# A fused block of sparse attention and routed experts: the order of statistics, masks, sums and weight pieces in its per-batch stage

## What is computed

```python
def xattn(h, adj, Wq, Wk, gamma_raw):                  # per batch, h = ctx, adj = layernorm(x)
    sim = einsum('bhnd,bhmd->bnm', Q, K) / (sqrt(32) * 4)
    threshold = top_k(sim, int(512 * 0.3))[0][:, :, -1:]   # the 153rd largest of each row
    A = sigmoid(sim) * (sim >= threshold)
    A = (A + swapaxes(A, -1, -2)) * 0.5
    gamma = sigmoid(gamma_raw)
    return (1.0 - gamma) * adj + gamma * A

x = x + tanh(g_xattn[0]) * xattn(ctx_512, layernorm(x), Wq, Wk, gamma_raw)
x = x + tanh(g_ffn[0]) * ffn(layernorm(x))     # shared silu(g) * y @ dw.T, and 2 of 8 experts by routing
```

## Time and profile before

| | us |
|---|---|
| median of 3 runs | 595.46 (594.64 to 596.95) |
| the profiled execution | 595.18 |
| its span, first to last instruction | 593.4 |
| attention of batch 0, up to the first shared block | 80.7 |
| stage of batch 1 | 62.0 |
| expert tiles | 258.7 |

### The profile page before, as it was taken

One profiled execution on the slowest core, in us unless ns is written; L12 is line 12 of the kernel. 1 busy time (PEld: TensorE's weight loads), 2 busy tenths in 40 slices (PEclk: granted clock), 3 DMA queues, 4 the chain that ended last, 5 costly groups with the idle time before them and its releaser, 6 DMA issues.

```text
span 593.4 us, 11085 instructions
## 1 busy us (share of the span) xinstructions
PE 507.4 (86%) x3169; PEld 289.1 (49%) x3170; DVE 343.6 (58%) x708; ACT 262.0 (44%) x473; POOL 232.2 (39%) x226
## 2 busy tenths in 40 slices
PE   2402589979998999879998899999999999999992
PEld 0100354434444454344464466666666666666660
DVE  0589758787868786977974377533333333333330
ACT  1696588646774579433231156322222222222221
POOL 1147735462446434550233034343343343443422
PEclk9655769989998999997999799999999999999997
DMA  3235293205611472034004489545445445445333
GB/s 113 97 91 173 80 305 108 57 30 182 250 42 36 138 275 57 21 106 147 1 1 159 149 230 242 123 77 95 79 75 95 78 78 96 74 77 97 74 43 46
DMA packets 32050, 63.75 MB, mean 107 GB/s; under 512 B 4049, under 2 KB 4305, under 8 KB 32017
## 3 DMA queue, kind: packets, MB, share of 16 engines
q1 hardware_dynamic: 23280, 42.89, 22.1%
q0 software_dynamic: 8736, 20.45, 18.9%
HBM read 41.05 MB, written 22.28 MB: 107 GB/s over the span
## 4 chain that ended last, share of the span: by engine, by line
PE 58%; DVE 17%; ACT 9%; issue 7%; DMA 5%; POOL 2%; SPq 1%; DVEq 1%; POOLq 0%; ACTq 0%
PE py L1004 12%; PE pg L984 12%; PE pu L985 12%; PE pg L845 4%; PE pu L845 4%; PE pt_bank L804 3%; DVE w L1178 3%; DVE pa L1137 3%; DVE w L1108 2%; PE pa L994 2%; PE py L862 2%; ACT w L613 2%; ACT w L619 2%; PE pu L862 2%; DVE w L1141 1%
## 5 line engine op out<-in xcount | busy, mean ns | idle before, releaser
L984 PE MATMUL pg<-w,x_t 128*128 x468 | 140.7, 313 | 0.0
L985 PE MATMUL pu<-w,x_t 128*128 x468 | 140.7, 313 | 0.0
L541 POOL DMA_INDIRECT out<-rows,idx x39 | 61.8, 1584 | 142.3 <-ACT rows L744 134.6
L1004 PE MATMUL py<-w,work 128*128 x351 | 82.1, 379 | 0.8 <-DVE work L1435 0.8
L845 PE MATMUL pg<-w 128*128 128x512 f16 (+1 forms) x288 | 80.2, 389 | 1.9 <-DVE work L1231 1.9
L845 PE MATMUL pu<-w 128*128 128x512 f16 (+1 forms) x288 | 79.7, 387 | 0.0
L734 ACT ACTIVATE work<-pg 128x352 f32<-128x352 f32 x39 | 18.0, 463 | 135.2 <-PE pu L985 135.2
L580 ACT ACTIVATE w<-stage 128x544 f16<-128x544 f32 (+1 forms) x80 | 50.7, 647 | 34.8 <-DMA stage<-in_weights 34.6
L488 POOL TENSOR_TENSOR w<-stage,w 128x544 f16<-128x544 f32 (+1 forms) x43 | 54.0, 1264 | 27.4 <-ACT stage L584 25.5
L494 POOL TENSOR_TENSOR work<-work 128x512 f16<-128x512 f32 (+1 forms) x24 | 29.0, 1209 | 81.9 <-ACT work L649 81.9
L1424 DVE SCALAR_TENSOR_TENSOR work<-pu,work 128x352 f32<-128x352 f32 x39 | 20.5, 524 | 62.6 <-ACT work L734 62.5
(11 more groups left out here) (189 smaller groups left out, 760.8 us busy)
## 6 DMA issues: line engine op xcount, KB each, us to landing
stage<-in_weights SPq DMA_DIRECT2D x80, 272.0 KB, 3.1
w<-in_x SPq DMA_DIRECT2D x4, 1024.0 KB, 6.6
out<-w SPq DMA_DIRECT2D x16, 256.0 KB, 2.8
xn_rows<-w SPq DMA_DIRECT2D x16, 256.0 KB, 5.3
out<-rows SPq DMA_DIRECT2D x13, 256.0 KB, 3.2
rows<-out SPq DMA_DIRECT2D x12, 256.0 KB, 3.0
w<-in_ctx_t SPq DMA_DIRECT2D x4, 256.0 KB, 3.4
out<-rows,idx POOLq DMA_INDIRECT x39, 4.7
```

The source lines that it names most:

```text
L541: pool.indirect_dma_start(out=out, out_offset=bass.IndirectOffsetOnAxis(ap=idx[:, t:t + 1], axis=0), in_=rows[:, t % 2, :], in_offset=None ...
L984: pe.matmul(pg[p][:, 0:H], lhs, w[:, item, half, at:at + H], start=begin, stop=end)
L985: mm = pe.matmul(pu[p][:, 0:H], lhs, w[:, item, half, at + H:at + 2 * H], start=begin, stop=end)
L1004: mm = pe.matmul(py[:, :], hid_t[:, p, part * JC + j, :], w[:, item, half, at:at + C], start=(j, part, half) == (0, 0, 0), stop=(j, part) ...
```

## The change

- **x.** Two buffers `xbs`, one of them in the place of weights item 6 (not yet loaded then), used by batch number. `load_x(1)` is issued behind `load_context(1)`, ahead of piece 8, the later ones behind the next context.
- **Masks.** They go to a buffer `kept` of their own, and ahead of the check for missed rows; the repair does its masks again. One release (`a_made`) per batch.
- **Sums.** `add_attention` is gone from POOL; DVE adds `kept` to x in `attended`.
- **x statistics.** `x_stats` comes behind the search in batch 0, and behind the first `shared_hidden` in the stages; `base` behind the searches, in the stages one block later than before.
- **Rows.** `statistics` of the sums and `row_scalars` by two tiles; ScalarE makes the high part in one pass straight from x, DVE the exact rows (`exact`) itself. DVE copies turned tiles 0 and 2, ScalarE 1 and 3.
- **Pieces.** `BY_DVE = 8`: DVE keeps 3 and 7 of the first 24. ScalarE does 16 pieces ahead of batch 0's rows instead of 20, and 8 behind `score_tanh(1)` instead of 4. POOL has `guess(1)` behind piece 17. PE waits for pieces as it needs them.
- **Loops.** The loop over the first two stages is written out on all engines.

```diff
-BY_DVE = 20
+BY_DVE = 8
-        xb = attn_tiles()
+        beside = w[:, EARLY - 1, :, :].rearrange("p b c -> p (b c)").bitcast(F32)
+        xbs = [beside[:, 0:TPB * SEQ].rearrange("p (i c) -> p i c", i=TPB), attn_tiles()]
+        kept = beside[:, TPB * SEQ:2 * TPB * SEQ].rearrange("p (i c) -> p i c", i=TPB)
...
             load_context(1, TPB)
+            load_x(1)
             for k in range(CHUNKS, last):
                 load_piece(k // CHUNKS, k % CHUNKS)
             sp.wait_ge(pad_st, 32)
             store_attended(0)
             store_rows(0)
-            load_x(TPB)
             load_piece(last // CHUNKS, last % CHUNKS)
... POOL
             first_pieces(0, FIRST)
-            add_attention(0)
-            first_pieces(FIRST, FIRST + 3)
-            row_scalars(0)
-            first_pieces(FIRST + 3, FIRST + 6)
+            row_scalars(0, 0)
+            row_scalars(0, 1)
+            first_pieces(FIRST, FIRST + 4)
             guess(1)
... POOL, stages
-                base_scalars(b + 1)
                 for u in range(UPS):
                     shared_low(b, u)
+                    if u == 1:
+                        base_scalars(b + 1)
                     if u < TPB:
                         low_piece(b + BEFORE, u)
-                add_attention(b + 1)
... ACT
             for n in range(ROUNDS):
                 count(0, n)
-                if n:
-                    base(0, (n - 1,))
                 high_piece(n // CHUNKS, n % CHUNKS)
-            base(0, (TPB - 1,))
-            for k in range(ROUNDS, FIRST + RING):
+            base(0)
+            for k in range(ROUNDS, FIRST + 2):
                 high_piece(k // CHUNKS, k % CHUNKS)
-            scores_and_rows(0, True, range(FIRST + RING, FIRST + RING + 2))
-            for k in range(FIRST + RING + 2, BEFORE * CHUNKS):
+            scores_and_rows(0, True)
+            for k in range(FIRST + 2, BEFORE * CHUNKS):
...
-                    if u == ROUNDS - 2:
+                    if u == ROUNDS - 1:
                         base(b + 1)
... DVE
+                for i in range(TPB):
+                    o.mark(keep(i))
                 after(dve, miss_mm, b + 1)
                 o.then(dve.tensor_copy(missed_i[:], pa[0][0:1, 0:1]))
...
+                for i in range(TPB):
+                    o.mark(dve.tensor_tensor(xbs[b % 2][:, i, :], kept[:, i, :], xbs[b % 2][:, i, :], ALU.add))
...
+                for i in (0, 2):
+                    if i:
+                        after(dve, xn_lo, b * TPB + i)
+                    made = [exact(i), exact(i + 1)]
+                    low_rows(i, made[0])
+                    low_rows(i + 1, made[1])
+                    if i == 0 and more:
+                        score_stats(b + 1, (0, 1))
+                    rows_turned(b, i)
...
             score_stats(0, range(TPB))
-            x_stats(0)
             for n in range(ROUNDS):
                 search(0, n)
+            x_stats(0)
             low_piece(0, 3)
...
-            masks(0, (1, 3))
-            low_piece(1, 7)
+            masks(0)
... DVE, stages
-                x_stats(b + 1)
                 search(b + 1, 0)
                 for u in range(UPS):
                     shared_hidden(b, u)
+                    if u == 0:
+                        x_stats(b + 1)
```

More of the change, by code:

```diff
@@ L385, in together @@
                 store_shared(tile0, 3)
-            with sp.Fori(0, BATCHES - 2) as b:
-                together(b, True)
-            together(BATCHES - 2, False)
+            for b in range(BATCHES - 1):
+                together(b, b + 2 < BATCHES)
             load_item(LATE)
@@ L525, in together @@
                 o.clear()
-            with pool.Fori(0, BATCHES - 2) as b:
-                together(b, True)
-            together(BATCHES - 2, False)
+            for b in range(BATCHES - 1):
+                together(b, b + 2 < BATCHES)
             for u in range(UPS):
@@ L649, in shared_high, with scores_and_rows @@
                 act.activation(hid_tb[0:m, u, 0, :], hb[0:m, u % 2, :], ACT.Copy).then_inc(hhi_sb, 1)
-            def scores_and_rows(b, more, pieces=()):
+            def scores_and_rows(b, more):
                 if more:
                     keep_qk(b + 1)
-                for k in pieces:
-                    high_piece(k // CHUNKS, k % CHUNKS)
                 for i in range(TPB):
@@ L703, in together @@
                 scores_and_rows(b + 1, more)
-            with act.Fori(0, BATCHES - 2) as b:
-                together(b, True)
-            together(BATCHES - 2, False)
+            for b in range(BATCHES - 1):
+                together(b, b + 2 < BATCHES)
             def router_exp():
@@ L832, in logits, with pieces_ready @@
                 mm.then_inc(lg_mm, 1)
+            def pieces_ready(n):
+                for r_, s in enumerate(w_lo):
+                    after(pe, s, len(range(r_, n, RING)))
+                after(pe, w_hi, n)
             def shared_up(b, u, beside=None, ks=range(KC)):
                 half, off, m = PIECES[u]
+                if b == 0 and 0 in ks and off == 0:
+                    pieces_ready(half * CHUNKS + -(-UP_W // CHUNK_W))
                 if u == 1 and beside is not None:
@@ L851, in shared_down @@
                 bank_ = down_bank(b, i)
+                if b == 0 and 0 in pieces and i == 0:
+                    pieces_ready(HALVES * CHUNKS)
                 if 0 in pieces:
@@ L878, in _ @@
                 turn_batch(0, i)
-            for s in w_lo:
-                after(pe, s, HALVES * (CHUNKS // RING))
-            after(pe, w_hi, HALVES * CHUNKS)
             pe.wait_ge(gw_ok, 1)
@@ L909, in together @@
                 turn_batch(b + 1, 3)
-            with pe.Fori(0, BATCHES - 2) as b:
-                together(b, True)
-            together(BATCHES - 2, False)
+            for b in range(BATCHES - 1):
+                together(b, b + 2 < BATCHES)
             def ranks():
@@ L1077, in low_piece, with statistics @@
                                          op0=ALU.mult, op1=ALU.subtract).then_inc(w_lo[n % RING], 1)
-            def statistics(s):
+            def statistics(s, tiles=range(TPB)):
                 o.wait()
-                for i in range(TPB):
+                for i in tiles:
                     o.mark(dve.bn_aggr(mv[:, s, i, :], bn6[:, s, i, :]))
@@ L1151, in count_missed, with masks, keep @@
                 o.then(dve.tensor_reduce(thr[:], hot8, AX.X, ALU.add))
-            def masks(b, piece=None):
+            def masks(b):
+                after(dve, sig_sb, (b + 1) * TPB)
+                after(dve, at_mm, b * TPB)
+                def keep(i):
+                    return dve.scalar_tensor_tensor(out=kept[:, i, :], in0=sim[:, i, :], scalar=thr[:, i:i + 1], in1=att[:, i, :],
+                                                    op0=ALU.is_ge, op1=ALU.mult)
+                for i in range(TPB):
+                    o.mark(keep(i))
                 after(dve, miss_mm, b + 1)
                 o.then(dve.tensor_copy(missed_i[:], pa[0][0:1, 0:1]))
-                if piece is not None:
-                    low_piece(*piece)
                 any_missed = dve.value_load(missed_i[0:1, 0:1], min_val=0, max_val=P * TPB)
@@ L1175, in masks @@
                         f.then(dve.tensor_copy(thr[:, i:i + 1], top8[:, i, (KEEP - 1) % 8:(KEEP - 1) % 8 + 1]))
-                after(dve, sig_sb, (b + 1) * TPB)
-                for i in range(TPB):
-                    dve.scalar_tensor_tensor(out=att[:, i, :], in0=sim[:, i, :], scalar=thr[:, i:i + 1], in1=att[:, i, :],
-                                             op0=ALU.is_ge, op1=ALU.mult).then_inc(a_made, 1)
+                        f.then(keep(i))
+                dve.sem_inc(a_made, 1)
             def attended(b, more, shared):
@@ L1273, in together @@
                 attended(b + 1, more, b)
-            with dve.Fori(0, BATCHES - 2) as b:
-                together(b, True)
-            together(BATCHES - 2, False)
+            for b in range(BATCHES - 1):
+                together(b, b + 2 < BATCHES)
             def bc(col):
```

144 lines of the change are left out of this document (73 added, 71 removed).

## The result

The changed kernel takes **621.03 us** (median of 4, 619.61 to 622.05) against 596.21 for the kernel before in the same rounds: ratio 1.045, 95% interval 1.041 to 1.050. It is slower by 4.5%, as forecast (616.0, range 604 to 626). Its profiled execution took 621.6 us.

The account below looks back on a forecast made before the run. Before 80.70 us TensorE mostly waits, and whatever moves the expert tiles' start moves the end. Third block 16.2 plus batches' 1.5, 1.1 and 2.0 gave 20.8, on 595.2: 616.0 us, range 604 to 626.

Parts of the forecast that it names:

- the head: Batch 0 up to its first transposes: late x statistics delay piece 7's low part by 7.0 us, the transposes by 6.5.
- From these transposes to the up-projection: Batch 0: 19.9 us instead of 18.7, so the up-projection starts at 88.4, 7.7 us late.
- the sums: Four new sums on VectorE in batch 0: 2.7 us, 1.5 of them beside the first transposes, so +1.2.
- I count nothing for all that together, bounds -2 and +2: Batch 0's rows: row scalars by halves, single-pass high rows, exact rows and score statistics together change nothing, within 2 us.
- The third block: Third up-block of batch 0: piece 23 waits behind eight stores, so it starts at 110.1 instead of 93.94, 16.2 us late.
- stores don't hold piece 23: Rival at the third block: it comes 10 us late instead of 16.2, 610 us in all; chance 0.15.
- The rounds of batches 1 to 3: Stages of batches 1 to 3: moved statistics, base activations, masks and sums cost +1.5, +1.1 and +2.0 us.
- the sums meet GpSimd: Rival in batches 2 and 3: GpSimd's pieces slow VectorE's sums, 4 us per batch, 624 us in all; chance 0.12.
- part 4: Rounds of batches 1 to 3: statistics +3.5, base activations -2.8 and +1.6, masks and check -0.8; batch 1 +1.5 us.
- The rule on exact rows: VectorE's exact rows: float32 tensor_scalar makes two results per cycle, so four take about 1.5 us instead of 3.

Follow-up runs that it names:

- e1: The changed kernel with x's statistics for batch 0 ahead of the four search rounds again: 611.33 us, ratio 1.030 to the kernel before.
- e7: e4 with the statistics of the first two score tiles behind the low rows of tiles 2 and 3: 599.97 us, ratio 1.008 to the kernel before.
- e2: The changed kernel with SyncE issuing weight piece 23 ahead of batch 0's eight stores: 615.16 us, ratio 1.039 to the kernel before.
- e3: The changed kernel with the weight pieces in their old places on ScalarE and GpSimd, x's statistics still late: 610.36 us, ratio 1.030.
- e10: The changed kernel with only the four sums of x and masked scores back on GpSimd: 612.68 us, ratio 1.031 to the kernel before.
- e5: e4 with the stages' old order: x's statistics and GpSimd's scalars at the head, base activations one block earlier: 594.71 us, ratio 1.000.
- e9: e4 with e5's order and e8's sums, so all costly moves undone: 585.53 us, ratio 0.984 to the kernel before.
- e12: e9 with the check of missed rows ahead of the four masks again, masks still in their own buffer: 591.5 us, ratio 0.996.
- e4: The changed kernel with e1 and e3 together: 600.04 us, ratio 1.010 to the kernel before.
- e8: e4 with the four sums back on GpSimd from the masks' own buffer, masks still ahead of the check: 593.52 us, ratio 0.998.

## Why the prediction was right, and where its terms were off

The first step, **the head**, held. The low parts start at 44.14 (said: 44.8), piece 7's low part at 54.47 (53.4), TensorE's third block at 110.88 (110.1). e1 shows that the place of x's statistics is the cause: with it undone, the first transposes come at 60.8. Inside, terms were off both ways. The search ended at 36.85, not 38.5: it begins 3.5 us earlier when the statistics aren't ahead of it (24.88 against 28.39), which the prediction left out, and its rounds took 12.0 us, not shorter for the base activations' absence. That bought nothing, as VectorE then waited 10.07 us for piece 7 instead of some 6. Piece 7 came 1.1 later than said. From there to the masks it took 5.7 us instead of the 8.3 kept from before. VectorE's steps had run beside GpSimd's low parts then, and now GpSimd stood idle for 7.25 us; the same two instructions before and after:

```profile
49.44 2.96 DVE L1137 SCALAR_TENSOR_TENSOR pa<-w 128x512 f32<-128x512 f16 x2
```

```profile
56.56 1.30 DVE L1136 SCALAR_TENSOR_TENSOR pa<-w 128x512 f32<-128x512 f16 x2
```

The masks took 4.66 instead of 5.7. So the first transposes were 4.2 us late, not 6.5.

**From these transposes to the up-projection** I took 19.9 us and it was 22.9, which gave the 2.3 back and 0.7 more. The term that failed is the sums: 2.7 us, because "in batch 0 GpSimd then stands at its row scalars". It didn't: with the pieces late, its six low parts ran from 61.13 for 9.2 us, beside masks and sums, and the sums took 5.32. In e1, where GpSimd did wait for its row scalars, they took 2.50, and from the transposes to the up-projection it was 20.1. For halves, exact rows and score statistics "I count nothing for all that together, bounds -2 and +2"; by e1 that held. A wait of 5.11 us does stand there at 85.83, but it stands in e1 too (5.10), and before the change TensorE waited 4.63 us for its turned rows at 74.44. The statistics' place is some 1.3 us of it (e7: 4.68 to 3.41). What makes the rest remains open; no run took it apart.

**The third block**: stores behind 96 us (97.75), issue 101.8 (103.30), landing 4 (3.4), count 107.1 (108.00), 16.2 late (16.9). The prediction's chain from 89.7 to 101.8 holds 0.8 us that it names no source for: its terms add up to 101.0. The rival that stores don't hold piece 23 is refuted by e2, which moved the block by 4.5 us. The other part of the wait went with e3, the places of the pieces.

**The rounds of batches 1 to 3** were the step that failed in size: 1.5 + 1.1 + 2.0 = 4.6 us said, and 3.4 + 3.7 + 3.3 = 10.4 measured. Two terms account for most of it. First, the sums. The prediction had them inside the 1.1 and 2.0, too small: e10 puts their place at 4.1 and 3.3 us in batches 2 and 3. The rival "the sums meet GpSimd" said 4 per batch at a chance of 0.12. Its price came out alike, but partly by luck: the sums took 4.57 and 4.28 us there, so meeting GpSimd added 1.9 and 1.6 to the 2.7 of sums alone, and the rest is that they stand in VectorE's queue at all. It was also wrong in adding it all to 616, since the masks fell from 5.22 to 2.73 us at the same time. Second, the clock, of which the prediction says nothing for the changed kernel: behind 9.89 us of waiting TensorE ran at the lower level of 1.2 GHz (the granted clock of 110.9 to 115.9 is 0.52 of full speed, of the same steps before 1.00). Three matmuls took 1.51 us against 0.85 before, and 5.01 us passed for the four groups of rows up to 115.89 that took 2.6 at the higher level. That alone is 2.4 us of batch 1's 3.4. The order of statistics and base activations, which part 4 priced step by step, can't be read from one stage: e5 gives it 5.3 us over all stages.

**The rule on exact rows** (the Trainium skill, VectorE: DVE Perf Modes, section Mode 2×_2P) is borne out in direction: a float32 multiply and add with row scalars took 0.53 to 0.54 us where nothing disturbed it (two in 1.00), not the 0.74 of the counting instruction. By the page's two results per cycle I had put four at 1.5 us; they took 2.0, between this and 3.

In all 20.8 us were said and 25.9 measured between the two profiled executions: the third block 0.7 too little, the rounds 5.8 too little, and 1.4 given back in the last stage and the tiles, of which the prediction says nothing. Some of the 1.4 is the clock again: the last stage's twelve matmuls took 4.12 us instead of 5.30. The largest term, and the direction, held by their mechanism. That the third block came within 0.7 us is in part luck, as the head's errors of -2.3 and +3.0 us cancelled; the rounds were said at less than half.

## What to carry to other kernels

A new buffer or a shorter step brings something only where the instruction that waits for it also stands where its early arrival can be used; ask of each moved instruction what its queue has behind it, above all on the engine that frees a ring of buffers. A queue in which the last piece of a stream stands behind a batch's stores makes that piece as late as the batch. And a change with several parts is worth taking apart: here all parts together cost 25 us, and those that were left when the costly moves were undone gained 10 on the kernel before.

## What the runs showed of the hardware

**The same matmuls after short waits.** The twelve matmuls behind the count of missed rows are the same in all kernels. After a wait of 0.48 us they took 2.75 us in every stage that had it (before, e5, e9, e12); after waits of 2.4 to 3.2 us they took from 2.75 to 5.28, in different stages of the same kernel:

```profile
122.34 4.08 PE L866 MATMUL pu<-w,work 128*128 128x512 f16 x12
...
188.02 2.75 PE L866 MATMUL pu<-w,work 128*128 128x512 f16 x12
...
252.41 5.28 PE L866 MATMUL pu<-w,work 128*128 128x512 f16 x12
```

(e4; its waits ahead of them are 2.98, 2.88 and 2.88 us.) The granted clock of these three stretches is 0.66, 1.00 and 0.50: in the third all twelve ran at the lower level, 1.2 GHz, in the second all at the higher, 2.4 GHz. By these rows a wait of 3 us can cost up to 5.5 (3 + 5.28 - 2.75, an estimate), and which stage pays changes from kernel to kernel. The last stage shows the same: behind a wait of 2.3 us its twelve matmuls took 2.77 us in e8 and 5.30 in e9. In e8 the three stages' twelve took 4.41, 5.28 and 4.34 us; with the waits gone, in e9, 2.75 each. Such stretches are thus part of what e9 gained over e8; how large a part of the median was not tested.

**VectorE beside GpSimd.** A mask took 0.74 us alone and up to 1.71, a sum 0.68 and up to 1.74 (L1196: 676, 1405 and 1737 ns as minimum, median and maximum of 16). Batch 0's four sums took 2.50 us with GpSimd idle (e1) and 5.32 beside its low parts. The sums' move from GpSimd to VectorE didn't end this contention, it changed which of VectorE's instructions met it. It works the other way too: GpSimd's power of 128x2 elements took 0.71 us by itself and 2.18 beside VectorE's exact and low rows (e12).
